# Softmax sums of the last attention pair divided among GpSimd, VectorE and TensorE, earlier scaling, weight loads in five cycles

## The chip, the cores and the metric

One core of one Trainium2 chip runs the whole program. The metric is the device time of one launch in microseconds (us).

## The reference

2048 rows of 256 attend with 16 heads of 64 to 1601 context rows of 192 and one null key; a feed-forward net of three layers follows. All is float32; L0_ffn weights are booleans that stand for 1 and -1.

```python
x = x + xattn(layernorm(x), ctx)
x = x + ffn(layernorm(x))

# xattn
q = layer_norm(x, g_norm) @ Wq;  k, v = split(ctx @ Wkv)     # 16 heads of 64, null key and value in front
attn = softmax(q @ k.T / 8)                                 # 2048 x 1602 for each head
out = layer_norm((attn @ v) @ Wout, g_out)

# ffn: w = where(k, 1, -1)
h = relu(s0 * concat(x, -x) @ w0) * 2;  h = relu(s1 * h @ w1) * 2;  return s2 * h @ w2
```

## The kernel before

Heads are done in 8 pairs. A pair has 4 query blocks (QB) of 512 queries, and each block has 13 key tiles (KT) of 128 keys, so a pair has 52 steps, two to a cycle: 26 cycles, c = 0 to 25. Over all pairs the blocks are counted 0 to 31; 30 and 31 are query blocks 2 and 3 of the last pair, pair 7. For every step TensorE makes the scores (L1361, 8 matmul calls), ACT takes the exponential of 128 x 1024 values (L833) into one of 8 slots of `prob`, and TensorE multiplies it with the values (L1374), one cycle later. A slot is written again 8 steps later, once its tile has been used by TensorE (`pv_done`) and by the adds (`sums_p`, through `freed_by`).

The sum under the softmax is taken over the key tiles first: GpSimd adds the 13 tiles of a block in 12 instructions (L647) into `acc`, and TensorE then sums `acc` over its partitions with a matmul by ones (L1310, `sums`). ACT copies the result (L744), SP stores it to memory and loads it spread out, VectorE inverts it (L1018), SP stores and broadcasts it, and the output of the block is multiplied by it: on GpSimd (L654, `normalise_o`), for block 31 on VectorE (L1025, `normalise_last`).

The order on each engine is written out by hand: tables (`K_AT`, `Q_AT`, `MX_AT`, `L_AT`, `C_AT`, `RECIP_AT`) give the cycle of each side job, and every engine runs through the same plan in order. Besides the steps, TensorE projects the next pair's keys and queries and finds maxima for the softmax shift (L1240), which VectorE reduces (L1005). In the last pair these maxima end in cycle 16, and the tail's work on rows 0 to 511 (block 0 of the tail) stands there instead: TensorE projects the attention output in cycles 17 and 18 (L1252), VectorE takes statistics (L1033 to L1038), GpSimd the roots (L659 to L664, `root_of_block_0(0)`, behind block 30's adds), ACT scales four tiles (L818, `scale_block_0(0)`, cycle 21), VectorE multiplies with gout, adds to x and takes statistics again (`attn_block_0`, L1061 to L1069, cycle 22), GpSimd the roots again (`root_of_block_0(1)`, after the seventh add of block 31), and ACT scales again (cycle 24). TensorE turns the result (L1384, `turn_block_0`), does the last two steps' values, and the tail begins.

ACT also issues the loads of the tail's weights (`load_ffn_weights`, L805 to L812, five DMA issues in cycle 22 of pair 6) and converts w1 in cycles 6 to 13 of pair 7. VectorE converts w0 (`split_small_weights`, L1077 and L1080) in cycle 17 of pair 7.

The tail has 4 blocks of 512 rows: a first layer of 8 tiles (4 matmuls each), a second of 8 tiles (16 each) and a third of 2 (16 each), all at L1464; ahead of the tiles of the second layer stands the attention output of the next block (L1436) and its turning. After each tile ACT does ReLU (L891, L892), and VectorE splits the result into a high and a low part (L1167, L1169); three PSUM banks (`f_free`) and two buffers (`h_free`) go round. In the tail's first block the second layer's tile 2 has the sums of block 31 in front of it (`sums(ps_last, ...)`, L1493) and their copy by ACT (`last_sums`, L884).

## Time and profile before

| | us |
|---|---|
| median of 3 runs | 1422.51 |
| the 3 runs | 1418.97, 1422.51, 1423.19 |
| the profiled execution | 1424.65 |
| its span | 1420.8 |
| TensorE busy (share of the span) | 1378.5 (97%) |
| GpSimd busy | 980.1 (69%) |
| VectorE busy | 695.2 (49%) |
| ACT busy | 641.0 (45%) |
| attention ends, tail begins (first L1464) | 1177.57 |

The profiled execution's 1424.65 us contain the span of 1420.8 us, in which the instructions lie; starts below are counted from the span's begin. "Idle before, releaser" is the time that an engine stood still ahead of an instruction and what ended it. TensorE's granted clock is 1.00 for 2.4 GHz and 0.50 for 1.2 GHz. POOL is GpSimd, DVE VectorE, PE TensorE, ACT ScalarE, ACTq ACT's queue of DMA issues.

### The profile page before, as it was taken

Reading aid. Unit: us, or ns where it says so; the run is one execution under the profiler, and the core shown is the slowest. Engines: PE = TensorE matmul, PEld = TensorE weight load, DVE = VectorE, ACT = ScalarE, POOL = GpSimd, SP = SyncE. Lnnn points to the kernel's source line nnn. Section 1 sums busy time; section 2 is a strip of 40 time slices with the busy share of each in tenths; the row PEclk is TensorE's granted clock in tenths of the full one; section 3 lists DMA queues with packets and bytes.
Section 4 is the critical chain, followed back from the end, with each engine's and each line's share of the span. In section 5 each row is a group of like instructions: output and inputs, shape, how many; then the busy total and the mean of one; then the engine's idle time right before and its main releaser. Section 6 shows DMA issues by size and latency. Waiting matters only on the chain.

```text
span 1420.8 us, 20714 instructions
## 1 busy us (share of the span) xinstructions
PE 1378.5 (97%) x7972; PEld 771.2 (54%) x7972; DVE 695.2 (49%) x961; ACT 641.0 (45%) x776; POOL 980.1 (69%) x495
## 2 busy tenths in 40 slices
PE   7999999999999999999999999999999998999998
PEld 3345555545545554555555545554455646877876
DVE  5445544545455554455545555454545624444542
ACT  4334444445544444454444444444456444333232
POOL 1028889888988998898899888988799974110100
PEclk9999999999999999999999999999999999999999
DMA  5240001000100010001001000100130220112000
GB/s 152 75 144 1 17 16 47 16 17 16 47 16 16 27 44 16 16 22 48 16 16 46 17 16 16 47 16 16 52 124 24 70 81 8 51 40 74 1 16 15
DMA packets 54998, 53.82 MB, mean 38 GB/s; under 512 B 13746, under 2 KB 41333, under 8 KB 54901
## 3 DMA queue, kind: packets, MB, share of 16 engines
q1 hardware_dynamic: 49044, 47.39, 10.9%
q10 hardware_dynamic: 5856, 5.11, 1.2%
q8 instruction: 63, 1.03, 0.3%
q14 instruction: 35, 0.28, 0.1%
HBM read 34.79 MB, written 17.56 MB: 37 GB/s over the span
## 4 chain that ended last, share of the span: by engine, by line
PE 83%; ACT 9%; POOL 3%; DVE 1%; issue 1%; DMA 1%; ACTq 0%; SPq 0%; DVEq 0%; POOLq 0%
PE ps_o L1374 26%; PE ps_s L1361 19%; ACT prob L833 8%; PE ps_x L1464 7%; PE ps_x L1240 7%; PE ps_s L1464 4%; PE ps_o L1293 4%; PE ps_s L1240 3%; POOL acc L647 3%; PE ps_s L1436 3%; PE ps_o L1310 2%; PE ps_s L1226 2%; PE ps_o L1282 2%; PE ps_o L1284 2%; PE ps_s L1228 2%
## 5 line engine op out<-in xcount | busy, mean ns | idle before, releaser
L647 POOL TENSOR_TENSOR acc<-acc,prob 128x1024 f32<-128x1024 f32 x352 | 838.7, 2383 | 94.3 <-ACT prob L833 51.8
L1005 DVE TENSOR_REDUCE mxh<-ps_x 128x2 f32<-128x804 f32 x408 | 407.0, 997 | 518.6 <-PE ps_x L1240 518.5
L833 ACT ACTIVATE prob<-ps_s,keybias 128x1024 f32<-128x1024 f32 x416 | 441.0, 1111 | 261.3 <-PE ps_s L1361 254.3
L1374 PE MATMUL ps_o<-prob,vp 128*64 128x512 f32 x1664 | 403.0, 605 | 1.5 <-DMA vp<-v_scratch 1.5
L1374 PEld LDWEIGHTS ps_o<-prob,vp 128*64 128x64 f32 x1664 | 100.8, 136 | 174.3 <-issue 167.0
L1361 PE MATMUL ps_s<-qh,kh 64*128 64x512 f32 x832 | 164.8, 392 | 3.2 <-ACT prob L833 3.2
L647 POOL TENSOR_TENSOR acc<-prob 128x1024 f32<-128x1024 f32 x32 | 76.0, 2374 | 128.9 <-issue 91.8
L1361 PE MATMUL ps_s<-ql,kh 64*128 64x512 f32 x832 | 164.5, 391 | 0.0
L1361 PE MATMUL ps_s<-qh,kl 64*128 64x512 f32 x832 | 164.4, 391 | 0.0
L1240 PE MATMUL ps_x<-kh,qh 64*128 64x402 f32 x816 | 162.4, 394 | 1.9 <-DVE mxh L1005 1.2
L1361 PE MATMUL ps_s<-shift,one_sel 64*128 64x512 f32 x832 | 163.6, 389 | 0.0
L1240 PEld LDWEIGHTS ps_x<-kh,qh 64*128 64x128 f32 x816 | 76.5, 184 | 156.6 <-issue 84.5
L1005 DVE TENSOR_REDUCE mxh<-ps_s 128x2 f32<-128x804 f32 x104 | 102.7, 988 | 5.2 <-PE ps_s L1240 5.2
L694 POOL TENSOR_TENSOR cve<-cmv,epscol 128x1 f32<-128x1 f32 x24 | 5.4, 224 | 143.6 <-DVE cmv L1122 118.6
L1361 PEld LDWEIGHTS ps_s<-qh,kh 64*128 64x128 f32 x832 | 78.7, 185 | 19.2 <-ACT prob L833 8.5
L1361 PEld LDWEIGHTS ps_s<-shift,one_sel 64*128 64x128 f32 x832 | 78.4, 184 | 18.5
L1361 PEld LDWEIGHTS ps_s<-ql,kh 64*128 64x128 f32 x832 | 78.2, 184 | 17.8
L1361 PEld LDWEIGHTS ps_s<-qh,kl 64*128 64x128 f32 x832 | 78.3, 184 | 8.7
L1464 PE MATMUL ps_x<-h0hi,w 128*128 128x512 f32 x160 | 64.4, 402 | 0.0
L1464 PE MATMUL ps_x<-h0lo,w 128*128 128x512 f32 x160 | 62.5, 390 | 0.0
L1293 PE MATMUL ps_o<-xT,wqp 128*64 128x512 f32 x256 | 60.6, 593 | 0.7 <-ACT xT L792 0.7
L726 ACT ACTIVATE qh<-ps_o 128x512 fp32r<-128x512 f32 x32 | 19.2, 599 | 83.3 <-PE ps_o L1293 83.3
(154 smaller groups left out, 1225.4 us busy)
## 6 DMA issues: line engine op xcount, KB each, us to landing
rb<-r_scratch SPq DMA_DIRECT2D x64, 128.0 KB, 2.9
o_scratch<-o_sb SPq DMA_DIRECT2D x32, 256.0 KB, 2.0
otb<-o_scratch SPq DMA_DIRECT2D x4, 2048.0 KB, 8.0
v_scratch<-vsb SPq DMA_DIRECT2D x13, 512.0 KB, 3.2
vp<-v_scratch SPq DMA_DIRECT2D x8, 832.0 KB, 5.0
xs<-in_x SPq DMA_DIRECT2D x4, 512.0 KB, 6.8
xres<-in_x ACTq DMA_DIRECT2D x1, 2048.0 KB, 9.8
out<-obuf SPq DMA_DIRECT2D x8, 256.0 KB, 2.2
```

Of the source, the lines that this page charges most:

```text
L647: gp.tensor_tensor(a, so_far, term, ALU.add).then_inc(sums_p, 1)
L833: act.activation(prob[:, slot(u, s), :, :], ps_s[s % S_BUFS][:, :, :], ACT.Exp, bias=keybias[:, kt:kt + 1], scale=SCALE).then_inc(p_made, 1)
L1005: dve.reduce_max(mxh[:, :, qt, quarter], ps[:, :, 0:MXW], AX.X).then_inc(x_free, 1)
L1226: pe.matmul(ps_v[h % 2], cT0[:, keys], wv0[:, cols], start=True, stop=False)
L1228: pe.matmul(ps_v[h % 2], cT1[:, keys], wv1[:, cols], start=False, stop=True).then_inc(vh_made, 1)
L1240: last = pe.matmul(ps[:, g, 0:MXW], qh[u][rows(g), (4 * qb + qt) * P:(4 * qb + qt + 1) * P], kh[u][rows(g), quarter * MXW:(quarter + 1) * ...
L1282: pe.matmul(ps[rows(g), 0:KCH], wkp0[nu][:, rows(g)], cT0[:, cols], start=True, stop=False)
L1293: last = pe.matmul(ps[rows(g), :], wqp[:, k, rows(g)], xT[:, k, cols], start=(k == 0), stop=(k == DC - 1))
L1361: last = pe.matmul(ps_s[s % S_BUFS][:, g, :], left[rows(g), cols], right[rows(g), moved], start=(left is kh[u] and right is qh[u]), stop=( ...
L1374: last = pe.matmul(ps_o[qb % 2][rows(g), :], vp[u][:, kt, rows(g)], prob[:, slot(u, s), g, :], start=(kt == 0), stop=(kt == KT - 1))
L1436: last = pe.matmul(ps_c[t % 2][:, 0:DIM], otb[:, k, t * P:(t + 1) * P], wo_sb[:, k, :], start=(k == 0), stop=(k == PAIRS - 1))
L1464: last = pe.matmul(ps_f[j % 3], weights(k)[:, m * P:(m + 1) * P], part[:, k, :], start=(k == 0 and part is hi), stop=(k == depth - 1 and p ...
```

## The change

- In block 30 VectorE sums tiles 2 to 5 with two reductions (`add_four`), into `acc_d`, and GpSimd adds the other tiles and, last, `acc_d` ("D"): 9 adds. In block 31 VectorE sums tiles 5 to 8, GpSimd adds tiles 0 to 4, 9 and 10 (6 adds), and TensorE sums `acc`, `acc_d` and tiles 11 and 12 itself, in `last_sums`, at the end of the last pair and no longer in the tail.
- ACT scales two tiles a cycle in cycles 19, 20 and 23, 24. GpSimd's roots stand ahead of tile 12 of block 30 and ahead of tile 9 of block 31. `attn_block_0` goes from cycle 22 to 20, `split_small_weights` from 17 to 18 and behind the statistics.
- Block 30's product with the reciprocal goes from GpSimd to VectorE, into the tail (`normalise_late`).
- ACT issues the five weight loads one a cycle in cycles 21 to 25 of pair 6, k1 first.

```diff
-YC, SUMS_P = 4, KT - 1
+BY_VECTOR = {QB * PAIRS - 2: (2, 3, 4, 5), QB * PAIRS - 1: (5, 6, 7, 8)}
+BY_TENSOR = {QB * PAIRS - 1: (11, 12)}
...
-def freed_by(s):
-    qb, kt = s // KT, s % KT
-    return SUMS_P * qb + max(kt, 1)
+def sums_of(b):
+    order = [kt for kt in range(KT) if kt not in BY_VECTOR.get(b, ()) + BY_TENSOR.get(b, ())]
+    return order + ["D"] if b in BY_VECTOR and b not in BY_TENSOR else order
+def sums_until(b):
+    return 1 + sum(len(sums_of(a)) - 1 for a in range(b))
+def freed_by(b, kt):
+    return sums_until(b) + max(sums_of(b).index(kt), 1)
...
+        at["sum"] = at["late"]
+        acc_d = sb("acc_d", [P, 2, QW], region="sum")
...
-        sums_p = sem("sums_p")
+        sums_p, sums_d = sem("sums_p"), sem("sums_d")
...
-                s = KT * qb + i
-                gp.wait_ge(p_made, S_BUFS + STEPS * n + s + 1)
-                term = prob[:, slot(u, s), :, :]
-                gp.wait_ge(sums_p, 1 + SUMS_P * b + i - 1)
+                kt = sums_of(b)[i]
+                if kt == "D":
+                    gp.wait_ge(sums_d, 2 * list(BY_VECTOR).index(b) + 2)
+                    term = acc_d[:, :, :]
+                else:
+                    gp.wait_ge(p_made, S_BUFS + STEPS * n + KT * qb + kt + 1)
+                    term = prob[:, slot(u, KT * qb + kt), :, :]
+                gp.wait_ge(sums_p, sums_until(b) + i - 1)
...
                 for qb in range(QB):
-                    for i in range(1, KT):
+                    order = sums_of(blocks(n, qb))
+                    for i in range(1, len(order)):
+                        if last and qb == 2 and order[i] == 12:
+                            root_of_block_0(0)
+                        if last and qb == 3 and order[i] == 9:
+                            root_of_block_0(1)
...
-                        if last and qb == 3 and i == 7:
-                            root_of_block_0(1)
...
-                    if last and qb == 2:
-                        root_of_block_0(0)
...
-                if last:
-                    normalise_o(n, 2)
...
-            def load_ffn_weights():
-                act.wait_ge(k_lo, 4 * PAIRS)
-                act.wait_ge(q_lo, QB * PAIRS)
-                act.dma_start(k0raw[:, :, :], k0.rearrange("(c p) n -> p c n", p=P)).then_inc(ld_raw, 16)
-                act.dma_start(k2raw[:, :, :], k2.rearrange("(c p) n -> p c n", p=P)).then_inc(ld_raw, 16)
-                act.dma_start(k1raw[:, :, :], k1.rearrange("(c p) n -> p c n", p=P)).then_inc(ld_raw, 16)
-                act.dma_start(gout[:, :], g_out.unsqueeze(0).broadcast_to([P, DIM])).then_inc(ld_gout, 16)
-                act.dma_start(wo_sb[:, :, :], wout.rearrange("(c p) n -> p c n", p=P)).then_inc(ld_wo, 16)
-            def scale_block_0(r):
+            def load_ffn_weights(i):
+                if i == 0:
+                    act.wait_ge(k_lo, 4 * PAIRS)
+                    act.wait_ge(q_lo, QB * PAIRS)
+                    act.dma_start(k1raw[:, :, :], k1.rearrange("(c p) n -> p c n", p=P)).then_inc(ld_raw, 16)
+                elif i == 1:
+                    act.dma_start(k0raw[:, :, :], k0.rearrange("(c p) n -> p c n", p=P)).then_inc(ld_raw, 16)
+                elif i == 2:
+                    act.dma_start(k2raw[:, :, :], k2.rearrange("(c p) n -> p c n", p=P)).then_inc(ld_raw, 16)
+                elif i == 3:
+                    act.dma_start(wo_sb[:, :, :], wout.rearrange("(c p) n -> p c n", p=P)).then_inc(ld_wo, 16)
+                else:
+                    act.dma_start(gout[:, :], g_out.unsqueeze(0).broadcast_to([P, DIM])).then_inc(ld_gout, 16)
+            def last_sums():
+                act.wait_ge(y_job_made, y_count(Y_LAST, LAST_PAIR) + 1)
+                act.wait_ge(s_stored, 32 * (QB * PAIRS - 1))
+                act.activation(s_sb[:, :], ps_last, ACT.Copy).then_inc(s_copied, 1)
+            def scale_block_0(r, tiles):
...
-                for t in range(4):
+                for t in tiles:
...
-                            act.wait_ge(sums_p, 1 + SUMS_P * QB * m + freed_by(old))
+                            b = blocks(m, old // KT)
+                            if old % KT in BY_VECTOR.get(b, ()):
+                                act.wait_ge(sums_d, 2 * list(BY_VECTOR).index(b) + 2)
+                            else:
+                                act.wait_ge(sums_p, freed_by(b, old % KT))
...
-                    if n == PAIRS - 2 and c == 22:
-                        load_ffn_weights()
+                    if n == PAIRS - 2 and c >= 21:
+                        load_ffn_weights(c - 21)
...
-                    if last and c == 21:
-                        scale_block_0(0)
-                    if last and c == 24:
-                        scale_block_0(1)
+                    if last and c in (19, 20):
+                        scale_block_0(0, range(2 * c - 38, 2 * c - 36))
+                    if last and c in (23, 24):
+                        scale_block_0(1, range(2 * c - 46, 2 * c - 44))
...
+                    last_sums()
...
-            def last_sums():
-                act.wait_ge(y_job_made, y_count(Y_LAST, LAST_PAIR) + 1)
-                act.wait_ge(s_stored, 32 * (QB * PAIRS - 1))
-                act.activation(s_sb[:, :], ps_last, ACT.Copy).then_inc(s_copied, 1)
...
-                    act.wait_ge(sums_p, 1 + SUMS_P * QB * PAIRS)
+                    act.wait_ge(sums_p, sums_until(QB * PAIRS))
...
-                    if start and m == 2:
-                        last_sums()
...
-            def normalise_last():
-                dve.wait_ge(r_loaded, 32 * QB * PAIRS)
-                dve.wait_ge(o_copied, QB * PAIRS)
-                dve.wait_ge(norm_done, QB * PAIRS - 1)
-                dve.tensor_tensor(o_sb[1][:, :], o_sb[1][:, :], rb[:, :], ALU.mult).then_inc(norm_done, 1)
+            def normalise_late(qb):
+                b = blocks(PAIRS - 1, qb)
+                dve.wait_ge(r_loaded, 32 * (b + 1))
+                dve.wait_ge(o_copied, b + 1)
+                dve.wait_ge(norm_done, b)
+                dve.tensor_tensor(o_sb[qb % 2][:, :], o_sb[qb % 2][:, :], rb[:, :], ALU.mult).then_inc(norm_done, 1)
+            def add_four(n, u, qb):
+                b = blocks(n, qb)
+                tiles = BY_VECTOR[b]
+                first = slot(u, KT * qb + tiles[0])
+                dve.wait_ge(p_made, S_BUFS + STEPS * n + KT * qb + tiles[-1] + 1)
+                if b == QB * PAIRS - 1:
+                    dve.wait_ge(sums_p, sums_until(b))
+                for g in range(2):
+                    dve.reduce_sum(acc_d[:, g, :], prob[:, first:first + 4, g, :].rearrange("p r q -> p q r"), AX.X).then_inc(sums_d, 1)
...
                     if last and c == C_AT[0]:
-                        split_small_weights()
+                        add_four(n, u, 2)
...
                     for qb in range(QB):
...
-                    if last and c == 22:
+                    if last and c == 18:
+                        split_small_weights()
+                    if last and c == 20:
...
+                    if last and c == 24:
+                        add_four(n, u, 3)
...
             def tail(b, with_next):
                 start = isinstance(b, int) and b == 0
...
-                    dve.wait_ge(sums_p, 1 + SUMS_P * (QB * PAIRS - 1) + freed_by(7))
+                    dve.wait_ge(sums_d, 4)
...
-                    dve.wait_ge(sums_p, 1 + SUMS_P * QB * PAIRS)
+                    dve.wait_ge(sums_p, sums_until(QB * PAIRS))
+                    dve.wait_ge(y_job_made, y_count(Y_LAST, LAST_PAIR) + 1)
                 for j in range(8):
...
+                    if start and j == 1:
+                        normalise_late(2)
...
-                        normalise_last()
+                        normalise_late(3)
...
-                pe.wait_ge(sums_p, 1 + SUMS_P * (blocks(n, qb) + 1))
+                pe.wait_ge(sums_p, sums_until(blocks(n, qb) + 1))
...
+            def last_sums(u):
+                b = QB * PAIRS - 1
+                pe.wait_ge(sums_p, sums_until(b + 1))
+                pe.wait_ge(sums_d, 4)
+                terms = [acc[(QB - 1) % 2], acc_d] + [prob[:, slot(u, STEPS - KT + kt), :, :] for kt in BY_TENSOR[b]]
+                for i, term in enumerate(terms):
+                    for g in range(2):
+                        last = pe.matmul(ps_last[rows(g), :], ones[:, :], term[:, g, :], start=(i == 0), stop=(i == len(terms) - 1))
+                last.then_inc(y_job_made, 1)
...
+                    last_sums(u)
...
-                        sums(ps_last, PAIRS - 1, QB - 1)
...
```

## Rows read from the trace of the kernel before

**Rows 1.** The page, part 1: busy time, share of the span, instructions of each engine.

```profile
PE 1378.5 (97%) x7972; PEld 771.2 (54%) x7972; DVE 695.2 (49%) x961; ACT 641.0 (45%) x776; POOL 980.1 (69%) x495
```

**Rows 2.** Timeline of ACT, pair 5: start us, us, engine, line, operation, [idle before <-releaser].

```profile
888.58 0.60 ACT L744 ACTIVATE s_sb<-ps_o 128x512 f32<-128x512 f32 x1 [2.28 <-PE ps_o L1310]
889.88 2.12 ACT L833 ACTIVATE prob<-ps_s,keybias 128x1024 f32<-128x1024 f32 x2 [0.69 <-PE ps_s L1361]
...
902.93 2.12 ACT L833 ACTIVATE prob<-ps_s,keybias 128x1024 f32<-128x1024 f32 x2 [2.15 <-PE ps_s L1361]
```

**Rows 3.** The same view, pair 6, with the weight loads.

```profile
1023.28 0.60 ACT L744 ACTIVATE s_sb<-ps_o 128x512 f32<-128x512 f32 x1 [2.28 <-PE ps_o L1310]
...
1025.74 2.43 ACTq L811 DMA_DIRECT2D gout<-in_L_xattn_g_out  x1
1028.20 1.76 ACTq L812 DMA_DIRECT2D wo_sb<-in_L_xattn_Wout  x1
...
1041.11 2.12 ACT L833 ACTIVATE prob<-ps_s,keybias 128x1024 f32<-128x1024 f32 x2 [2.14 <-PE ps_s L1361]
```

**Rows 4.** Timeline of TensorE, end of the last pair and first tail block.

```profile
1166.97 0.50 PE L1361 MATMUL ps_s<-qh,kh 64*128 64x512 f32 x2
...
1169.03 1.94 PE L1374 MATMUL ps_o<-prob,vp 128*64 128x512 f32 x8
1173.74 1.06 PE L1384 MATMUL ps_x<-ident,y 128*128 128x128 f32 x8 [2.78 <-ACT y L818]
...
1177.57 0.47 PE L1464 MATMUL ps_x<-yhi,w 128*128 128x512 f32 x1 [0.84 <-issue]
...
1185.27 0.50 PE L1464 MATMUL ps_s<-yhi,w 128*128 128x512 f32 x1 [2.88 <-ACTq L894]
...
1195.47 0.58 PE L1464 MATMUL ps_s<-h0hi,w 128*128 128x512 f32 x1
```

**Rows 5.** Timeline of ACT, the second scaling.

```profile
1171.52 2.07 ACT L818 ACTIVATE y<-xres,y0nm,y0rs 128x256 f32<-128x256 f32 x4 [5.13 <-POOL y0nm L664]
```

**Rows 6.** Timeline of GpSimd (POOL), last block.

```profile
1152.97 16.60 POOL L647 TENSOR_TENSOR acc<-acc,prob 128x1024 f32<-128x1024 f32 x6
1169.66 0.23 POOL L659 TENSOR_SCALAR y0var<-y0mv 128x4 f32<-128x4 f32 x1
...
1171.44 12.40 POOL L647 TENSOR_TENSOR acc<-acc,prob 128x1024 f32<-128x1024 f32 x5
```

**Rows 7.** Timeline of VectorE (DVE), last pair.

```profile
1117.92 11.07 DVE L1080 TENSOR_TENSOR w<-k0raw 128x512 fp32r<-128x512 uint8 x4
...
1142.23 0.24 DVE L1038 BATCH_NORM_AGGREGATE y0mv<-y0st 128x2 f32<-128x6 f32 x2
1155.75 3.20 DVE L1061 TENSOR_TENSOR y<-y,gout 128x1024 f32<-128x1024 f32 x1 [13.29 <-ACT y L818]
...
1164.42 0.20 DVE L1018 RECIPROCAL r<-s 128x8 f32<-128x8 f32 x1 [0.28 <-DMA s<-s_scratch]
```

**Rows 8.** One line's instructions: durations in ns min/median/max, first and last start.

```profile
L1066 DVE BATCH_NORM_STATS2 y0st<-xres x4: 409/409/428, 1162.3 to 1163.3; 128x6 f32<-128x256 f32 x4
...
L1169 DVE TENSOR_TENSOR h0lo<-hf,h0hi x8: 691/693/2731, 1181.7 to 1192.6; 128x512 fp32r<-128x512 f32 x8
```

**Rows 9.** Busy time in one stretch; after the engines the granted clock (PEclk).

```profile
1187.50:1193.00 5.50, 5.48 (x13) 4.35 (x14) 3.94 (x7) 3.91 (x6) 0.00 (x0) 0.50 0.00 0
```

**Rows 10.** Chain of waits: start us, us, engine, tile, line, count.

```profile
1140.72 1.87 PE ps_o L1374 x8
...
1199.47 3.45 PE ps_s L1436 x16
```

**Rows 11.** The page, part 5: group of instructions, busy us, mean ns, idle before.

```profile
L1005 DVE TENSOR_REDUCE mxh<-ps_x 128x2 f32<-128x804 f32 x408 | 407.0, 997 | 518.6 <-PE ps_x L1240 518.5
```

**Rows 12.** Timeline of ACT, ReLU of the first layer.

```profile
1187.60 0.69 ACT L892 ACTIVATE hf<-ps_x,scol 128x512 f32<-128x512 f32 x1 [0.17 <-ACT hf L892]
...
1189.90 0.69 ACT L892 ACTIVATE hf<-ps_x,scol 128x512 f32<-128x512 f32 x1 [0.17 <-ACT hf L892]
```

## The prediction, made before the changed kernel was run

> **What bounds the kernel now.** I read the page first: TensorE is busy for 97% of the span [rows 1]. VectorE and GpSimd matter only where they make it wait. The table of waits puts nearly all that TensorE waits in the last attention pair and the first tail block down to ACT (the releasers in [rows 4] show it), so I followed ACT's waits back through the timelines, in two places.
>
> First place: late in pair 6 ACT issues five weight loads in one lump. In the undisturbed pair 5 ACT goes from its copy of the sums (cycle 22) to the exponentials of the next pair's cycle 0 in 902.93 - 888.58 = 14.35 us [rows 2]; in pair 6 the same way takes 1041.11 - 1023.28 = 17.83 us [rows 3]. The lump costs 3.48 us and nothing later gives it back.
>
> Second place: the seam between attention and tail [rows 4]. TensorE ends the values of cycle 24 at 1169.03 + 1.87 = 1170.90, and turns y at 1173.74 only: a wait for ACT's second scaling, and that for GpSimd (5.13 us of idle time before it [rows 5]). GpSimd has the roots behind a run of adds: it begins them at 1169.66 [rows 6], although VectorE had its statistics by 1164.14 (it then waited 0.28 us for the sums, until 1164.42 [rows 7]). After the roots GpSimd still has five adds, until 1171.44 + 12.40 = 1183.8 [rows 6], and block 30's product behind them. In that time VectorE's subtraction of two SBUF operands takes up to 2.73 us, against 0.69 us at the median of the same line [rows 8]. ReLU waits for VectorE, TensorE for ReLU: a wait of 2.88 us ahead of tile 5 of the first layer [rows 4], a further one, and then a stretch at a granted clock of 0.50, which is 1.2 GHz instead of 2.4 GHz, behind these waits [rows 9]. The first matmul of the second layer comes at 1195.47, 17.9 us after the first of the first layer at 1177.57 [rows 4].
>
> **The change part by part.** GpSimd's blocks 30 and 31 (query blocks 2 and 3 of the last pair) go from 12 adds each to 9 and 6, so 9 fewer. Its adds take 16.60 / 6 = 2.77 us [rows 6].
>
> **Loads spread out.** The same five issues, one in each of cycles 21 to 25. The longest are 2.43 us (gout, now cycle 25) and 1.76 us (wout, cycle 24) [rows 3]; behind a cycle's exponentials ACT is idle for 2.15 us [rows 2] and 0.69 us in the tightest cycle, 22, which gets the short k0 load. gout overruns by 0.3 us, and TensorE needs an exponential only two steps later, so it is covered; without that cover it costs 0.3. The bytes land spread over about 20 us, with ld_raw wanted in cycle 6 of pair 7. SP's small transfers for sums, reciprocals and shift share the DMA engines before and after. Gain 3.5; bounds 2.5 (one small transfer late by 1 us) and 3.5.
>
> **Scaling earlier.** VectorE now first does the four sums of block 30 at 1117.9, where the w0 conversion stood. That conversion took 11.07 us there and only then came the statistics of the first product [rows 7], so anything up to 11 us is covered. The conversion moves behind the second product's statistics (end 1142.47 [rows 7]): with GpSimd adding, it ends at 1153.5 at the latest. The attention output of block 0 then takes 1164.14 - 1155.75 = 8.4 us [rows 7]: statistics by 1161.9. GpSimd's root now stands before tile 9, behind the adds of tiles 1 to 4. Before, the fourth add ended near 1152.97 + 3 x 2.77 = 1161.3 [rows 6]. The first roots, which now stand ahead of tile 12 of block 30, wait for the statistics of 1142.47, and behind them are tile 12, VectorE's part and the product: about 1 us later than now, so 1162. The roots take 1171.44 - 1169.66 = 1.8 us [rows 6]: 1163.8. ACT scales two tiles (2.07 / 2 = 1.0 us [rows 5]) and one exponential takes 1.06 (2.12 for two [rows 2]): 1165.9. TensorE wants that one at 1166.97 [rows 4]: the reserve is about 1 us. The other two tiles are scaled in cycle 24, by 1168.5, before TensorE can turn y at 1170.90. So the wait of 1173.74 - 1170.90 = 2.84 us goes.
>
> **The last sums.** Turning y and the last values took 1177.57 - 0.84 - 1173.74 = 2.99 us [rows 4], so they end at 1173.9. Now come 8 matmul calls, 16 matmuls in the trace (each call of this type shows as two), of the form of which 8 take 1.87 us [rows 10]: 3.74 us, to 1177.6. They are queued ahead of the first layer. They need GpSimd's tile 10 (its exponential ends near 1167.5, two adds behind it: about 1172) and VectorE's four sums of block 31. The copy to yhi and the subtraction, for which TensorE waited 0.84 us, hide beside them. **The first layer starts at 1177.6, as before: the 2.84 us and the 0.84 us are paid back in matmuls.**
>
> **VectorE's four sums.** No row has a reduction out of SBUF over four tiles. The nearest is its reduction of 804 elements out of PSUM in 997 ns [rows 11]; by size 2048 elements take 2.54 us, two of them 5.1 us a block. I take that, because statistics, also one input, but out of SBUF, took 409 ns for 256 elements while GpSimd was adding [rows 8]; that rate would make it 3.3. Block 31's begin at 1164.6, behind the reciprocal at 1164.42 [rows 7], and end at 1169.7, with 1173.9 as the limit: cost nothing. The lower end is no cost either, the upper is the rate of the w0 conversion, two SBUF inputs beside GpSimd: four instructions of 512 elements in 11.07 us, 5.4 ns an element [rows 7], 11.1 us a reduction. The Trainium skill speaks against this form: Vector Engine (DVE) Microarchitecture Reference, section 5.2, has a source that hops 4 KiB with every element, as these do, at 1.73 instead of 1.05 ns a column. As an estimate by that page a reduction takes 3.6 us and block 31's end at 1171.8; the sum stays as it is, the reserve halves, and the slow rival below gains a little. No row here shows it.
>
> **First layer.** With GpSimd done VectorE is at its short times. ReLU starts then follow at 2.30 us for two tiles (1187.60 to 1189.90 [rows 12]), and TensorE needs 7.4 us for the eight tiles (32 matmuls at 1.87 / 8 = 0.23 [rows 10]). Its tile 7 waits for the bank of tile 4: 1.3 (first tile done) + 2 x 2.30 + 0.7 = 6.6, and with its own 0.9 and latencies the layer ends 7.8 us after its start. The output projection follows, 3.45 us for 16 matmuls at full clock [rows 10]: the second layer starts 11.2 us after the first instead of 17.9: gain 6.7, with bounds of 4.1 (the half clock returns, 2.6: projection and three tiles at half speed) and 7.5.
>
> **Sums taken out of the tail.** 4 matmuls of the same form ahead of tile 10: gain 0.9. **Products on VectorE.** Block 30's product moves from GpSimd to VectorE in the tail: one more subtraction-sized instruction, 0.69 us, in a stretch where VectorE waits for TensorE; SP's stores of the output and the sums come a little earlier than now, since the sums are copied before the first layer. Nothing.
>
> **Sum:** 3.5 + 0 + 6.7 + 0.9 = 11.1 us. The profiled execution took 1424.65 us (span 1420.8), which would give 1413.5; it lies 2.1 above the median of 1422.51, and by the median it is **1411.4**.
>
> **The rivals.** (a) **The wait moves into the scaling chain.** The reserve is 1 us, and GpSimd's adds stretch when VectorE runs two-input operations. If the roots are 2 us later, exponential 48 and with it the scores of cycle 25, the last sums and the tail are 1 to 3 us later: 1412.5 to 1414.5. For it: GpSimd's six adds there average 2.77 us, its five after the roots 12.40 / 5 = 2.48 [rows 6]. Against: it has fewer adds. Chance 0.2. (b) **The slow VectorE isn't GpSimd's doing,** so that taking adds away leaves the waits in the first layer. Then only loads and tail sums count: 4.4 us, 1418.1. For it: only two subtractions show it. Against: most of the line's subtractions in this stretch, those that come after GpSimd's adds, take 0.69. Chance 0.07. (c) **The other side: the strided reduction is slow.** At 11.1 us each block 30's pair ends at 1140.0 instead of 1129.0, and the statistics, products and all behind them come up to 11.0 later; block 31's ends at 1186.7, 12.8 us after TensorE wants it. Against 11.1 gained that is 1.7 to 12.7 slower, about 1430. It decides from (1173.9 - 1164.6 + 11.1) / 2 = 10.2 us a reduction; under 4.6 it costs nothing. For it: VectorE's slow rows beside GpSimd; against: its one-input row is not slow. Chance 0.05. (d) The forecast: 0.68.
>
> **How the numbers follow.** About 0.3% (4.3 us) can be told from no change. The forecast and (a) are faster, (b) lies on the edge and is split, (c) is slower, with a little more for what I have not seen: faster 0.89, same 0.06, slower 0.05. The range runs from all upper bounds (11.9 us, and 2.6 for the scatter of the runs shown, 1418.97 to 1423.19) to (b) and 1 us of scatter: 1408 to 1419.
>
> **What would show it.** Right: no wait of TensorE in cycle 23 of pair 6; turning y within 0.1 us of the values before it; 16 sums matmuls in 3.7 us, then the first layer with waits under 0.5 us, all at clock 1.00, and the second layer about 11 us after the first; reductions of 2.5 to 3.3 us. Wrong: a wait ahead of the scores of cycle 25 or of the last sums, VectorE's subtraction at over 2 us in the first layer, a clock of 0.50 there, or reductions over 4.6 us.

## The result and the profile after

| | before | after |
|---|---|---|
| median, us | 1422.55 (6 runs, 1418.97 to 1423.19) | 1411.3 (6 runs, 1411.00 to 1411.73) |
| ratio to before, 95% interval | | 0.9926, 0.9913 to 0.9939 |
| profiled execution, us | 1424.65 | 1411.73 |
| its span | 1420.8 | 1409.9 |
| GpSimd busy | 980.1 | 957.2 |
| first matmul of the first layer | 1177.57 | 1174.37 |
| first matmul of the second layer | 1195.47 | 1185.49 |

The change saves 11.2 us; 11.1 were forecast. Line numbers moved: the exponential is L863, the values L1416, turning y L1437, the last sums L1428, the layers L1518, GpSimd's adds L664, VectorE's reductions L1060, its subtraction L1208. The profiled execution is 0.67 us later than that of before when it reaches cycle 22 of pair 6 (1023.95 against 1023.28), a difference from parts that the change doesn't touch.

Timeline of ACT after the change, pair 6, to [rows 2, 3]:

```profile
1023.95 0.60 ACT L759 ACTIVATE s_sb<-ps_o 128x512 f32<-128x512 f32 x1 [2.28 <-PE ps_o L1352]
1024.65 0.37 ACTq L826 DMA_DIRECT2D k0raw<-in_L_ffn_k  x1
...
1030.68 0.37 ACTq L830 DMA_DIRECT2D wo_sb<-in_L_xattn_Wout  x1
...
1034.95 0.35 ACTq L832 DMA_DIRECT2D gout<-in_L_xattn_g_out  x1
...
1038.30 2.12 ACT L863 ACTIVATE prob<-ps_s,keybias 128x1024 f32<-128x1024 f32 x2 [2.16 <-PE ps_s L1403]
```

From the copy of the sums to the exponentials of cycle 0 it is 1038.30 - 1023.95 = 14.35 us, to the hundredth what the undisturbed pair needs [rows 2]: 3.48 us gone. Each issue takes 0.35 to 0.42 us, also those for gout and wout that took 2.43 and 1.76 in the lump [rows 3].

Timeline of TensorE, to [rows 4]:

```profile
1166.18 1.94 PE L1416 MATMUL ps_o<-prob,vp 128*64 128x512 f32 x8
1168.05 1.09 PE L1437 MATMUL ps_x<-ident,y 128*128 128x128 f32 x8
1169.07 1.94 PE L1416 MATMUL ps_o<-prob,vp 128*64 128x512 f32 x8
1170.84 1.03 PE L1428 MATMUL ps_s<-acc,ones 128*64 128x512 f32 x4
...
1174.37 0.50 PE L1518 MATMUL ps_x<-yhi,w 128*128 128x512 f32 x1
...
1185.49 0.58 PE L1518 MATMUL ps_s<-h0hi,w 128*128 128x512 f32 x1
```

TensorE turns y right behind the values of cycle 24, with no wait. The last sums begin at 1170.84 and take 3.53 us, the layer follows at once, and the second layer comes 11.12 us after the first. All waits of TensorE that the profile lists between 1000 and 1300 us (releaser, us in total, times, longest):

```profile
PE ps_o L1560 <- DVEq L1236: 1.1, 4, 0.4
PE ps_s L1518 <- ACTq L919: 0.5, 1, 0.5
PE ps_x L1518 <- ACTq L919: 0.3, 1, 0.3
```

None of them lies before 1236 us: those of the first line begin at 1236.16, with the turning of the first tail block's output, and the other two (at 1240.52 and behind) stand in the second block's first layer. The last pairs and the first block's first layer have none. The granted clock stays at 1.00 in that layer (busy time of PE, PEld, DVE, ACT, POOL, then PEclk), to [rows 9]:

```profile
1174.00:1186.00 12.00, 11.88 (x54) 9.33 (x51) 7.26 (x13) 8.42 (x13) 0.00 (x0) 1.00 0.00 0
```

Timelines of GpSimd and of VectorE, to [rows 6, 7, 8]:

```profile
1115.92 9.91 POOL L664 TENSOR_TENSOR acc<-acc,prob 128x1024 f32<-128x1024 f32 x4 [8.26 <-ACT prob L863]
1131.09 4.85 POOL L664 TENSOR_TENSOR acc<-acc,prob 128x1024 f32<-128x1024 f32 x2 [5.25 <-ACT prob L863]
...
1150.90 9.05 POOL L664 TENSOR_TENSOR acc<-acc,prob 128x1024 f32<-128x1024 f32 x3
1160.04 0.23 POOL L676 TENSOR_SCALAR y0var<-y0mv 128x4 f32<-128x4 f32 x1
...
1164.07 4.92 POOL L664 TENSOR_TENSOR acc<-acc,prob 128x1024 f32<-128x1024 f32 x2 [2.20 <-ACT prob L863]
```

```profile
1115.00 7.55 DVE L1060 TENSOR_REDUCE acc_d<-prob 128x512 f32<-128x2048 f32 x2
...
1139.78 2.49 DVE L1115 TENSOR_TENSOR w<-k0raw 128x512 fp32r<-128x512 uint8 x4
1148.48 3.37 DVE L1096 TENSOR_TENSOR y<-y,gout 128x1024 f32<-128x1024 f32 x1 [6.21 <-ACT y L844]
...
1160.58 7.58 DVE L1060 TENSOR_REDUCE acc_d<-prob 128x512 f32<-128x2048 f32 x2
...
1176.46 0.43 DVE L1206 CAST h0hi<-hf 128x512 fp32r<-128x512 f32 x1 [5.67 <-ACT hf L917]
1176.93 0.69 DVE L1208 TENSOR_TENSOR h0lo<-hf,h0hi 128x512 fp32r<-128x512 f32 x1
```

GpSimd ends its last add at 1169.0, before the layer, and VectorE's cast and subtraction are at 0.43 and 0.69 us from the first tile on. The w0 conversion, 11.07 us beside GpSimd's adds [rows 7], takes 2.49 us here, where GpSimd has only its small root instructions. In block 30 GpSimd stands idle for 8.3, 5.3 and 3.8 us.

**Where the 10.9 us of the span came from:** loads 3.48, the start of the first layer a further 0.39 (1177.57 + 0.67 - 3.48 - 1174.37), first to second layer 17.90 - 11.12 = 6.78, and 0.92 behind that, from the second layer's first matmul to the end of the span ((1420.8 - 1195.47) - (1409.9 - 1185.49)); less 0.67 for the later start: 10.9.

### The profile page after: what moved, and what is told of

It is laid out like the page before. It is cut to its first block, busy times and chain, and to the rows that moved or that the text cites. A ratio compares the mean times of both kernels' runs of the same rounds, so it can differ in the third digit from the quotient of the medians.

```text
span 1409.9 us, 20726 instructions
## 1 busy us (share of the span) xinstructions
PE 1378.2 (98%) x7984; PEld 772.6 (55%) x7984; DVE 697.4 (49%) x966; ACT 640.6 (45%) x776; POOL 957.2 (68%) x485
## 4 chain that ended last, share of the span: by engine, by line
PE 88%; ACT 9%; issue 1%; DMA 1%; DVE 1%; SPq 0%; DVEq 0%; ACTq 0%
PE ps_o L1416 28%; PE ps_s L1403 21%; ACT prob L863 7%; PE ps_x L1518 7%; PE ps_x L1282 7%; PE ps_s L1518 4%; PE ps_o L1335 4%; PE ps_s L1282 3%; PE ps_s L1490 3%; PE ps_o L1352 2%; PE ps_s L1268 2%; PE ps_o L1324 2%; PE ps_o L1326 2%; PE ps_s L1270 2%; PE ps_x L1294 1%
## 5 line engine op out<-in xcount | busy, mean ns | idle before, releaser
L664 POOL TENSOR_TENSOR acc<-acc,prob 128x1024 f32<-128x1024 f32 x342 | 814.3, 2381 | 96.8 <-ACT prob L863 55.8
L863 ACT ACTIVATE prob<-ps_s,keybias 128x1024 f32<-128x1024 f32 x416 | 440.6, 1111 | 255.1 <-PE ps_s L1403 255.1
L1416 PE MATMUL ps_o<-prob,vp 128*64 128x512 f32 x1664 | 402.9, 605 | 1.5 <-DMA vp<-v_scratch 1.5
L1416 PEld LDWEIGHTS ps_o<-prob,vp 128*64 128x64 f32 x1664 | 100.9, 136 | 174.3 <-issue 165.3
L664 POOL TENSOR_TENSOR acc<-prob 128x1024 f32<-128x1024 f32 x32 | 75.9, 2372 | 129.1 <-issue 92.1
L1518 PE MATMUL ps_x<-h0hi,w 128*128 128x512 f32 x160 | 64.3, 402 | 0.0
L1518 PE MATMUL ps_x<-h0lo,w 128*128 128x512 f32 x160 | 62.4, 390 | 0.0
```

The lines of the kernel that those rows point to most:

```text
L664: gp.tensor_tensor(a, so_far, term, ALU.add).then_inc(sums_p, 1)
L863: act.activation(prob[:, slot(u, s), :, :], ps_s[s % S_BUFS][:, :, :], ACT.Exp, bias=keybias[:, kt:kt + 1], scale=SCALE).then_inc(p_made, 1)
L1416: last = pe.matmul(ps_o[qb % 2][rows(g), :], vp[u][:, kt, rows(g)], prob[:, slot(u, s), g, :], start=(kt == 0), stop=(kt == KT - 1))
L1518: last = pe.matmul(ps_f[j % 3], weights(k)[:, m * P:(m + 1) * P], part[:, k, :], start=(k == 0 and part is hi), stop=(k == depth - 1 and p ...
```

## The experiments

Medians; the ratios to the kernel before on the same chip have intervals of about 0.0015 to either side, some 2 us. The changed kernel is 1411.3.

| run | median, us | range | runs |
|---|---|---|---|
| e1, loads in a lump again | 1415.3 | 1413.72 to 1417.26 | 4 |
| e2, before with the loads spread | 1417.8 | 1416.59 to 1418.34 | 5 |
| e3, five more adds on GpSimd | 1416.8 | 1416.15 to 1417.99 | 4 |
| e4, second roots and scaling late | 1417.0 | 1416.24 to 1417.63 | 5 |
| e5, more reductions | 1411.9 | one | 1 |
| e6, no VectorE part in block 30 | 1410.9 | 1410.30 to 1411.13 | 4 |
| e7, no TensorE part | 1414.6 | 1413.84 to 1415.03 | 4 |
| e8, TensorE takes tile 12 alone | 1410.8 | 1410.00 to 1411.88 | 4 |
| e9, e8 with the sums inside the layer | 1410.5 | 1409.99 to 1410.79 | 5 |
| e10, no tile for TensorE, sums inside the layer | 1409.7 | 1409.42 to 1410.30 | 4 |
| e11, no sums on VectorE | 1414.2 | 1414.12 to 1414.61 | 4 |
| e12, e6 and e8 together | 1410.0 | 1409.71 to 1411.14 | 5 |

### e1: the loads in a lump again

```diff
-                    if n == PAIRS - 2 and c >= 21:
-                        load_ffn_weights(c - 21)
+                    if n == PAIRS - 2 and c == 22:
+                        load_ffn_weights()          # the old function: k0, k2, k1, gout, wout
```

> The changed kernel with one part undone: the five weight loads in one lump again, in cycle 22 of pair 6 and in the old order. Theory (loads and seam are two separate gains, 3.5 and 7.4 us): 1411.3 + 3.5 = 1414.8 us, ACT's way from its copy of the sums (cycle 22) to the exponentials of the next pair's cycle 0 at 17.8 us again, the seam as in the changed kernel. Rival (the lump was hidden, and what the loads gave came from the seam): 1411 to 1412.

Measured 1415.3, so 4.0 us more than the changed kernel. Timeline of ACT and granted clock in this run:

```profile
1024.08 0.60 ACT L759 ACTIVATE s_sb<-ps_o 128x512 f32<-128x512 f32 x1 [2.28 <-PE ps_o L1347]
...
1026.54 3.53 ACTq L826 DMA_DIRECT2D gout<-in_L_xattn_g_out  x1
1030.10 0.46 ACTq L827 DMA_DIRECT2D wo_sb<-in_L_xattn_Wout  x1
...
1043.19 2.12 ACT L858 ACTIVATE prob<-ps_s,keybias 128x1024 f32<-128x1024 f32 x2 [2.17 <-PE ps_s L1398]
```

```profile
1030.00:1035.00 5.00, 3.15 (x16) 2.55 (x18) 0.00 (x1) 3.37 (x4) 2.99 (x2) 0.72 1.08 344
```

The gout issue takes 3.53 us here and wout 0.46; in the kernel before gout took 2.43 and wout 1.76 [rows 3]. So that time is not gout's own: it comes with the three issues ahead of it, and spread out it does not exist. From the copy of the sums to the exponentials of cycle 0 it is 1043.19 - 1024.08 = 19.11 us, 4.76 more than in the changed kernel and 1.3 more than I expected. After the lump TensorE waited 2.95 us for an exponential, and in this execution ran at half clock for part of the next 5 us (0.72 on average); in the profiled execution of before the same wait, 3.2 us, left the clock at 1.00. The four runs of e1 lie 3.5 us apart, the six of the changed kernel 0.7. A half clock that comes in some executions and not in others would fit that, but only the profiled executions show the clock, and it can't be all: two of e1's runs, 1413.72 and 1414.24, are less than 3.48 us above the changed kernel. That stays open. The rival (the lump is hidden) is out.

### e2: the kernel before, with the loads spread

```diff
 # kernel before
-                    if n == PAIRS - 2 and c == 22:
-                        load_ffn_weights()
+                    if n == PAIRS - 2 and c >= 21:
+                        load_ffn_weights(c - 21)    # the new function
```

> The kernel before with one part of the change alone: the five weight loads spread over cycles 21 to 25 of pair 6. Theory: 1422.5 - 3.5 = 1419.0 us, the seam as before, with its waits of 2.8, 0.8, 2.9 and 1.0 us and the stretch at a granted clock of 0.50. Rival (the gains overlap: with the loads spread the seam is late by less): under 1417.

Measured 1417.8: 4.6 us less than the kernel before on the same chip (1422.42), 1.2 less than I expected, and above the rival's 1417. In its trace the clock falls at another place than before, already when y is turned (timeline of TensorE, then the clock of a stretch):

```profile
1170.65 1.94 PE L1389 MATMUL ps_x<-ident,y 128*128 128x128 f32 x8 [2.80 <-ACT y L823]
1172.52 3.68 PE L1379 MATMUL ps_o<-prob,vp 128*64 128x512 f32 x8
```

```profile
1171.00:1176.00 5.00, 5.00 (x16) 1.96 (x14) 1.29 (x2) 2.47 (x4) 4.71 (x3) 0.50 0.02 3
```

Turning and values take 1176.13 - 1170.65 = 5.48 us here instead of 2.98 in the kernel before, and the first layer's wait is 2.35 us instead of 2.88 and 1.05. In sum the way from the values of cycle 24 (1165.91) to the second layer (1191.27) is 25.36 us instead of 26.44. The way from the copy of the sums to the exponentials of cycle 0 is 14.35 us, as in the changed kernel. So the loads give 3.48 us here, and the 1.1 us beyond them lie in the seam, where the clock fell at another place. In the medians of this run and e1 spreading the loads brings 4.0 to 4.6 us, and the rest of the change 6.6 to 7.1.

### e3: five more adds on GpSimd beside the first layer

```diff
+            gp.wait_ge(w1_made, FK)
+            gp.wait_ge(y_job_made, y_count(Y_LAST, LAST_PAIR))
+            for k in range(5):
+                gp.wait_ge(sums_p, sums_until(QB * PAIRS) + k)
+                gp.tensor_tensor(acc[0][:, :, :], acc[0][:, :, :], w1[1 + k][:, :]..., ALU.add).then_inc(sums_p, 1)
...
-                    act.wait_ge(sums_p, sums_until(QB * PAIRS))      # ahead of the second layer
+                    act.wait_ge(sums_p, sums_until(QB * PAIRS) + 5)
-                    dve.wait_ge(sums_p, sums_until(QB * PAIRS))
+                    dve.wait_ge(sums_p, sums_until(QB * PAIRS) + 5)
```

> The changed kernel with one thing added: after its last add of block 31 GpSimd does five more adds of 128 x 1024 (acc of block 30, no longer needed, plus converted weights), which nothing but the end of the first layer waits for. They run from about 1169 to 1181.5, as far into the first layer as the old ones did. Theory (VectorE is slow because GpSimd adds): VectorE's cast goes from 0.43 to about 2 us and its subtraction from 0.69 to 2.2 to 2.7 for the first tiles, TensorE waits ahead of tiles 5 and 6, the half clock may come back, and the time rises by 4 to 7 us, to 1415 to 1418. Rival (b) of the prediction (the slowness is not GpSimd's doing): VectorE at 0.43 and 0.69, time 1411.3.

Measured 1416.8: 5.5 us more. Timelines of GpSimd, VectorE and TensorE:

```profile
1168.52 12.75 POOL L710 TENSOR_TENSOR acc<-acc,w 128x1024 f32<-128x1024 f32 x5 [0.17 <-POOL acc L664]
```

```profile
1175.81 0.43 DVE L1212 CAST h0hi<-hf 128x512 fp32r<-128x512 f32 x1 [5.67 <-ACT hf L923]
1176.28 5.55 DVE L1214 TENSOR_TENSOR h0lo<-hf,h0hi 128x512 fp32r<-128x512 f32 x2
...
1182.19 0.69 DVE L1214 TENSOR_TENSOR h0lo<-hf,h0hi 128x512 fp32r<-128x512 f32 x1
```

```profile
1179.93 0.50 PE L1524 MATMUL ps_s<-yhi,w 128*128 128x512 f32 x1 [1.35 <-ACTq L925]
...
1183.28 0.80 PE L1524 MATMUL ps_x<-yhi,w 128*128 128x512 f32 x1 [2.16 <-ACTq L925]
```

ACT's ReLU in between, and the clock of the stretch:

```profile
1181.92 0.69 ACT L922 ACTIVATE h0hi<-ps_x,scol 128x512 fp32r<-128x512 f32 x1 [2.09 <-DVE h0lo L1214]
```

```profile
1180.00:1185.00 5.00, 2.84 (x8) 2.03 (x9) 4.44 (x6) 2.74 (x5) 1.27 (x1) 0.79 0.00 0
```

The adds end at 1181.3. Until then two subtractions take 5.55 us, from then on 0.69 each; one cast, at 1175.81, stayed at 0.43. ReLU itself stays at 0.69 us a tile, but it stands 2.09 us for VectorE's subtraction; TensorE waits 1.35 and 2.16 us for ReLU, and the clock is 0.79 on average behind. First to second layer: 1189.88 - 1173.73 = 16.15 us instead of 11.12. Nothing waits for these adds before the layer's end, and the only instructions that grew while they ran are VectorE's subtractions: the theory holds, rival (b) of the prediction is out.

### e4: second roots and scaling late

```diff
-                        if last and qb == 3 and order[i] == 9:
-                            root_of_block_0(1)
                         add(n, u, qb, i)
+                        if last and qb == 3 and order[i] == 10:
+                            root_of_block_0(1)
...
-                    if last and c in (23, 24):
-                        scale_block_0(1, range(2 * c - 46, 2 * c - 44))
+                    if last and c == 24:
+                        scale_block_0(1, range(4))
```

> The changed kernel with the order of the scaling undone for its second part: GpSimd's roots stand behind its last add of block 31 and ACT scales all four tiles in cycle 24. Theory (the place of the roots on GpSimd sets when TensorE can turn y): roots begin near 1169 and end near 1170.8, ACT scales until 1172.9, TensorE turns y at about 1173 and not at 1168.05, ACT's last two exponentials come behind, and the time rises by about 5 us to 1416.5. Rival (there is slack behind the turning, since the last sums of 3.6 us can run first or the first layer is bound by ReLU): 1411 to 1413.

Measured 1417.0: 5.7 us more. Timeline of ACT, timeline of TensorE and clock:

```profile
1168.64 2.07 ACT L844 ACTIVATE y<-xres,y0nm,y0rs 128x256 f32<-128x256 f32 x4 [5.94 <-POOL y0nm L681]
```

```profile
1170.85 1.94 PE L1437 MATMUL ps_x<-ident,y 128*128 128x128 f32 x8 [3.59 <-ACT y L844]
1172.72 3.68 PE L1416 MATMUL ps_o<-prob,vp 128*64 128x512 f32 x8
```

```profile
1170.00:1175.00 5.00, 4.15 (x14) 2.33 (x16) 1.29 (x2) 3.68 (x6) 0.00 (x0) 0.50 0.02 3
```

TensorE waits 3.59 us and then turns y and does two steps' values at half clock, 5.3 us instead of 2.8. There is no slack behind the turning. The place of the roots on GpSimd sets the time as the theory says; I had expected the wait longer and no half clock.

### e5: the reduction, four apart and four together

```diff
+ # six times in cycle 17, after VectorE's four sums and after the first product's statistics
+ view = otb[:, 0:8:2, 0:384].rearrange("p r q -> p q r")                        # hop: 4 KiB apart
+ view = otb[:, 0:3, :].rearrange("p r q -> p (r q)").rearrange("p (q r) -> p q r", r=4)   # near
+ dve.reduce_sum(extra[:, :], view, AX.X)
```

> The changed kernel with six more reductions on VectorE in cycle 17 of the last pair, all of 128 x 1536 to 128 x 384 values, sums of four: three read four elements that lie 4 KiB apart (hop), three read four neighbours (near). Two stand while GpSimd adds, four where it mostly rests. In the changed kernel one of the 2048-element reductions took 3.78 us, against 2.54 forecast. If the hop is the cause (the page's rule): hop 3.78 x 3/4 = 2.8 us, near about 1.7 us, GpSimd adding or not. If GpSimd's adds are the cause: near and hop alike slow beside GpSimd, and both near 1.7 us at rest. If any four-to-one reduction is slow: all near 2.8 us. The time itself says nothing here.

Durations of the extra instructions in three stretches (ns min/median/max, first and last start): near and then hop beside GpSimd's adds, which end at 1125.56, inside the hop; hop with GpSimd at rest until 1130.80; hop beside GpSimd and near with GpSimd at rest:

```profile
L1074 DVE TENSOR_REDUCE extra<-otb x2: 1741/2292/2842, 1122.2 to 1123.9; 128x384 f32<-128x1536 f32 x2
```

```profile
L1074 DVE TENSOR_REDUCE extra<-otb x1: 2898/2898/2898, 1128.5 to 1128.5; 128x384 f32<-128x1536 f32 x1
```

```profile
L1074 DVE TENSOR_REDUCE extra<-otb x2: 1753/2303/2853, 1133.2 to 1136.1; 128x384 f32<-128x1536 f32 x2
```

Near takes 1.74 beside GpSimd and 1.75 at rest, hop 2.84 and 2.85 beside it and 2.90 at rest. The hop is the cause, and GpSimd is none. That is the rule of the Trainium skill (Vector Engine (DVE) Microarchitecture Reference, section 5.2): it has 1.73 ns a column for a source that hops 4 KiB with each element. This run has 2.87 / 1536 = 1.87 ns and the kernel's own reductions 3.78 / 2048 = 1.85, both with the fixed part, so the trace agrees in kind and to 7 or 8% in size.

### e6: no VectorE part in block 30

```diff
-BY_VECTOR = {QB * PAIRS - 2: (2, 3, 4, 5), QB * PAIRS - 1: (5, 6, 7, 8)}
+BY_VECTOR = {QB * PAIRS - 1: (5, 6, 7, 8)}
...
-                    if last and c == C_AT[0]:
-                        add_four(n, u, 2)
...                    # both waits for sums_d go from 4 to 2
```

> The changed kernel without VectorE's part in block 30: GpSimd adds all its 13 tiles again (12 adds). Theory (GpSimd catches up in block 30 while TensorE does the two products of cycles 17 and 18, in the changed kernel it stands idle there for 8.3, 5.3 and 3.8 us): no wait appears, and the roots for block 31 even come up to 2.5 us earlier; 1411.3, within 0.5. Rival (taking work off GpSimd in block 30 is what keeps the seam free): roots later, exponential 48 later, 1412.5 to 1415.

Measured 1410.9, no more than the changed kernel; the 0.4 us less are within the scatter. GpSimd's roots begin 2.5 us earlier than in the changed kernel (1160.04), as its timeline shows:

```profile
1157.53 0.23 POOL L676 TENSOR_SCALAR y0var<-y0mv 128x4 f32<-128x4 f32 x1
```

The part is not needed: GpSimd spends on the four tiles what it otherwise stands idle, and the add of `acc_d` at the end of the block delays it. The rival is out.

### e7: no TensorE part

```diff
-BY_TENSOR = {QB * PAIRS - 1: (11, 12)}
+BY_TENSOR = {QB * PAIRS - 1: ()}
```

> The changed kernel without TensorE's part: GpSimd adds tiles 11 and 12 of block 31 too, TensorE sums acc and acc_d only (8 matmuls in the trace, 1.8 us, instead of 16). Theory: GpSimd's last add ends 5 us after 1169.0, near 1174; TensorE, done with the values at 1170.84, waits 3.1 us for it, then 1.8 us of sums, so the first layer starts near 1175.8 instead of 1174.4 and the time is 1412.7. VectorE is not disturbed in the first layer. Rival (the 3.6 us of TensorE sums are a plain loss, GpSimd would have been in time): 1409.5. A second one: the wait of 3 us brings the half clock, then 1414 to 1415.

Measured 1414.6, with the wait and with the half clock (timeline of TensorE, clock):

```profile
1173.86 1.08 PE L1428 MATMUL ps_s<-acc,ones 128*64 128x512 f32 x4 [3.02 <-POOL acc L664]
```

```profile
1175.00:1180.00 5.00, 5.00 (x16) 3.01 (x13) 0.75 (x2) 1.83 (x3) 0.00 (x0) 0.66 0.01 3
```

The second rival, which is the theory with the clock added, gives the number. TensorE's two tiles are worth 3.3 us although they cost it 1.8 us of matmuls.

### e8, e9, e10 and e12: candidates

```diff
 # e8
-BY_TENSOR = {QB * PAIRS - 1: (11, 12)}
+BY_TENSOR = {QB * PAIRS - 1: (12,)}
...
-                pe.wait_ge(sums_p, sums_until(b + 1))
                 pe.wait_ge(sums_d, 4)
-                terms = [acc[(QB - 1) % 2], acc_d] + [prob[...] for kt in BY_TENSOR[b]]
+                terms = [acc_d] + [prob[...] for kt in BY_TENSOR[b]] + [acc[(QB - 1) % 2]]
                 for i, term in enumerate(terms):
+                    if i == len(terms) - 1:
+                        pe.wait_ge(sums_p, sums_until(b + 1))
 # e9: as e8, and last_sums (TensorE, ACT's copy too) between tiles 4 and 5 of the first layer
+                    if start and m == 5:
+                        last_sums((PAIRS - 1) % 2)
 # e10: as e9, with
+BY_TENSOR = {QB * PAIRS - 1: ()}
 # e12: e6 and e8 together
```

> A candidate: TensorE takes tile 12 alone, GpSimd adds tile 11, and the last sums begin with acc_d and tile 12 and end with acc, for which alone they wait. GpSimd ends near 1171.4, TensorE wants acc at 1172.6. Theory: 4 matmuls fewer and no wait: 1411.3 - 0.9 = 1410.4. Rival (GpSimd's add is later than that, or reaches into VectorE's subtraction for ylo, which the first layer needs): 1411 to 1412.

> A candidate on top of the one with tile 12 alone for TensorE: the last sums (12 matmuls in the trace, 2.6 us) stand between tiles 4 and 5 of the first layer instead of ahead of it. Theory: the layer is paced by ReLU (2.3 us for two tiles against TensorE's 1.84), the sums fill what TensorE waits there (0.8 us), but the layer now needs ylo as soon as the values end, some 0.2 us of wait: 1410.2. Rival (the wait for ylo is the longer one, or the copy of the sums holds up ReLU): 1411 or more.

> As the run before, but GpSimd adds tiles 11 and 12 (until about 1174) and TensorE sums acc_d and acc only, between tiles 4 and 5 of the first layer. TensorE has 4 matmuls fewer (0.9 us) than with tile 12. Theory: GpSimd is done before TensorE comes to the sums, but its last add lies beside VectorE's first cast and subtraction, which then take 1 to 2 us longer; ReLU's pace has that much to spare only in part: 1409.5 to 1411. Rival (overlap of even one add costs more than 4 matmuls): over 1411.

> A candidate: no VectorE part in block 30, TensorE takes tile 12 alone in block 31 and sums acc last. The run without VectorE's part in block 30 gave 1410.9 and the one with tile 12 alone 1410.8. Theory (the first costs and gives nothing, the second gives 0.9 less scatter): 1410.4, no waits of TensorE ahead of the first layer. Rival: the two together bring GpSimd's tile 11 no earlier and the time stays at 1410.9 to 1411.3.

e8 gives 1410.8: TensorE comes to acc at 1171.59 and GpSimd's last add ended at 1170.5, so there is no wait, but of the 0.9 us only 0.5 show in the median, within the scatter of the runs. The traces show it better: from turning y to the second layer it is 17.44 us in the changed kernel and 16.57 in e8. e9 gives 1410.5 and 16.52 us on that way, so moving the sums into the layer gains nothing. Its expectation rested on a misreading: the 0.8 us of waits that the sums were to fill lie in the second tail block (from 1240.52 in the changed kernel, 1239.61 in e9), not in the first. e12 gives 1410.0 and 16.58 us: less than its theory's 1410.4 and below its rival's 1410.9, though one of its five runs took 1411.14. e10 is the best with 1409.7 and 15.68 us; all its runs lie below all of the changed kernel's, by 1.6 us in the median and 1.76 on that way in the trace, though the two were timed on different chips, with the kernel before at 1422.45 and 1422.55. Timelines of GpSimd and of VectorE in e10:

```profile
1163.60 9.99 POOL L664 TENSOR_TENSOR acc<-acc,prob 128x1024 f32<-128x1024 f32 x4 [2.20 <-ACT prob L863]
```

```profile
1172.56 1.32 DVE L1207 CAST h0hi<-hf 128x512 fp32r<-128x512 f32 x1 [2.24 <-ACT hf L916]
1173.91 1.29 DVE L1209 TENSOR_TENSOR h0lo<-hf,h0hi 128x512 fp32r<-128x512 f32 x2
```

GpSimd's last add ends at 1173.6, and VectorE's first cast, beside it, takes 1.32 us instead of 0.43. (Not every cast beside an add is slowed: the one at 1175.81 in e3 was not.) One such overlap is cheaper than four matmuls on TensorE. e10 without the VectorE part in block 30 was not tried.

### e11: no sums on VectorE at all

```diff
-BY_VECTOR = {QB * PAIRS - 2: (2, 3, 4, 5), QB * PAIRS - 1: (5, 6, 7, 8)}
+BY_VECTOR = {}
...
-                        if last and qb == 3 and order[i] == 9:
+                        if last and qb == 3 and order[i] == 7:
                             root_of_block_0(1)
...
-                terms = [acc[(QB - 1) % 2], acc_d] + [prob[...] for kt in BY_TENSOR[b]]
+                terms = [prob[...] for kt in BY_TENSOR[b]] + [acc[(QB - 1) % 2]]    # waits for acc ahead of the last term
```

> The changed kernel without any sums on VectorE: GpSimd adds all tiles of block 30 and tiles 0 to 10 of block 31 (10 adds), TensorE sums tiles 11 and 12 and, last, acc; the roots for the second scaling stand ahead of tile 7. Theory (VectorE's four tiles of block 31 are what lets GpSimd end early): GpSimd's four adds more take 10 us, its last add ends near 1174, roots near 1164; exponential 48 and the turning come 1 to 2 us late, TensorE then waits for acc: 1413 to 1415, perhaps with the half clock. Rival (GpSimd alone would do, once its roots are well placed): under 1412.

Measured 1414.2, 2.9 us more. Timelines of GpSimd and of TensorE:

```profile
1148.20 14.25 POOL L664 TENSOR_TENSOR acc<-acc,prob 128x1024 f32<-128x1024 f32 x5
1162.53 0.23 POOL L676 TENSOR_SCALAR y0var<-y0mv 128x4 f32<-128x4 f32 x1
```

```profile
1166.54 0.79 PE L1399 MATMUL ps_s<-qh,kh 64*128 64x512 f32 x2 [2.72 <-ACT prob L863]
...
1176.30 1.03 PE L1424 MATMUL ps_s<-acc,ones 128*64 128x512 f32 x4
```

The wait is 2.72 us ahead of the scores of cycle 25, because the roots begin at 1162.53. The wait for acc that I had expected too does not come: TensorE is so much later that it reaches acc at 1176.30, 2 us after GpSimd's last add. With this order VectorE's part in block 31 is needed, and for the scaling more than for the sums. A better order was not tried: VectorE's statistics ended at 1154.49 here, so with the roots two tiles earlier (ahead of tile 5) they could begin near 1157, as in e6, and the wait of 2.72 us should go. GpSimd's last add would still end at 1174.2. On e6's times TensorE would want acc at about 1170.5 + 1.8 = 1172.3, a wait of some 2 us, against 0.9 us for four matmuls fewer. That is an estimate; how much VectorE's part in block 31 is worth stays open, between it and the 2.9 us measured.

## Why the prediction was right

The mechanism came out as forecast: the waits that were to go went, and e1, e3 and e4 bring them back one by one. That forecast and median agree to 0.1 us is luck: by the medians of e1 and e2 the loads gave 0.5 to 1.1 us more than forecast and the rest 0.5 to 1.0 less, and in the profiled executions 0.39 us at the layer's start stand against a start that was 0.67 us later.

**Loads (3.5 forecast).** In the trace 3.48. In the medians 4.0 (e1) and 4.6 (e2), more than the upper bound of 3.5 that I gave. In e1's trace the lump costs 4.76 us instead of 3.48, since a stretch at half clock follows the wait; that was not in my bounds. In e2's trace the surplus lies in the seam. The step on the issues was wrong: gout does not overrun its cycle by 0.3 us, since it takes 0.35 us when nothing is queued ahead. It made no difference.

**Scaling earlier.** The wait of 2.84 us went, as forecast, and rival (a) stayed away, but by less than I had thought. The first exponential of cycle 24 ended at 1162.90 + 1.05 = 1163.95 and TensorE began its next scores at 1164.12: a reserve of under 0.2 us instead of 1. On the clock of before (2.85 us later, by the values of cycle 24: 1169.03 and 1166.18) GpSimd's roots began at 1162.9 and not at 1162, because three of its adds took 9.05 us beside VectorE's products. e6 has 2.5 us more of reserve.

**The last sums and the start of the layer.** Forecast: paid back exactly, the layer as late as before. Measured: 3.53 us for the sums instead of 3.74, the layer 0.39 us earlier, without the loads. e7 shows that the payment was right.

**VectorE's four sums.** The mis-sized term: 3.78 us a reduction (7.55 for two) instead of 2.54, beyond the 3.3 of the statistics row too. The nearest row was a reduction with neighbours as its elements; the hop costs a further 0.7 ns an element. They ended at 1168.2, TensorE asked at 1170.84: hidden, as forecast, and rival (c) was far from its 10.2 us.

**First layer (6.7 forecast).** 6.78 measured. e3 brings 5.03 of it back with nothing but adds on GpSimd (the output projection ran at full clock there, 3.62 us, and took 4.72 in the kernel before), so the cause is shown and not only argued: VectorE beside GpSimd, ReLU behind VectorE, TensorE behind ReLU, and the clock behind TensorE's waits.

**Sums out of the tail (0.9).** Behind the second layer's start the changed kernel is 0.92 us shorter. That holds this term together with the product of block 30, which I had put at nothing; no run has either alone.

**Block 30's part on VectorE**, which I counted as covered, is covered and also useless (e6).

## What to carry to other kernels

When an engine off the critical path shares the SBUF with one that is close to it, look at the same instruction beside and away from the other's work: here 2.7 against 0.69 us, and 11.1 against 2.5. Moving work away from that stretch was worth more than the matmuls that it cost, but only where someone was late: of three places to which adds were moved, block 30's gave nothing. Issue large loads one at a time between an engine's instructions; in a lump the later issues stand behind the earlier ones and hold the engine.

## What the hardware showed that I had not expected

- The granted clock after a wait of TensorE of about 3 us varies. It stayed at 1.00 behind waits of 3.2 and 2.8 us in the profiled execution of before, and fell to 0.50 behind 2.80 us (e2) and 3.59 us (e4); stretches behind 2.72 us (e11), 2.95 us (e1) and 3.02 us (e7) had 0.66, 0.72 and 0.66 on average, and the one behind e3's 1.35 and 2.16 us 0.79. Turning and two steps' values then take 5.3 to 5.5 us instead of 2.8, so a wait can cost up to 2.7 us on top of itself. The scatter of the runs does not tell such kernels from others: e1 has 3.5 us and the kernel before 4.2, but e11 0.5, and e8, without such a wait, 1.9.
- The w0 conversion, four subtractions of uint8 into 512 values each, takes 2.49 us with GpSimd nearly at rest and 11.07 us beside its adds, a factor of 4.4. The roots on GpSimd beside it took 2.6 us instead of 1.8.
- An issue of a weight load takes 0.35 to 0.42 us by itself; behind three others one took 2.43 us in one execution and 3.53 us in another.
- One-input reductions are not slowed by GpSimd at all (1.74 and 1.75 us), but by a source that hops 4 KiB with each element (2.87). A subtraction with one input from PSUM and one from the SBUF was not slowed either: the two for ylo take 1.29 us beside e3's adds, as in the changed kernel, where GpSimd rests.
